# Choosing the tokens: one unit of the experts' first layer behind each block's gate products

## The reference

```python
gate_scores = softmax(x @ w_gate_w + w_gate_b)          # 8 experts
mask = one_hot(top_k(gate_scores, 2)).sum(-2)
masked = gate_scores * mask
route = masked / (masked.sum(axis=0) + EPS) * capacity  # over the 4 rows of the batch
_, seq_ids = top_k(route.transpose(2, 0, 1), S // 2)    # each expert takes 512 of 1024 tokens of a row
h = gelu(xg @ W1 + b1)                                  # 64 hidden numbers for each expert
o = h @ W2 + b2
outs = zeros.at[flat_ids].add(o)
```

## Time and profile before

| | |
|---|---|
| median of 3 runs | 3541.02 us (3540.13 to 3545.2) |
| profiled execution | 3554.61 us |
| its span, first to last instruction | 3552.9 us |
| mean granted clock of TensorE | 0.92 |
| TensorE (PE) busy | 3169.2 us, 89% |
| VectorE (DVE) busy | 2786.6 us, 78% |
| ScalarE (ACT) busy | 2104.8 us, 59% |
| `choose` in it | 3347.9 to 3463.2 us |
| `take` in it | 3463.2 to 3552.9 us |

### The profile page before, as it was taken

The page is one execution under the profiler, slowest core; times in us unless marked ns, Lnnn a source line. Parts: engine busy times, 40 slices in busy tenths (PEclk is TensorE's granted clock), DMA queues, the critical chain, the costliest instruction groups (busy, mean ns, idle before and its releaser), DMA issues. The chain is left out here.

```text
span 3552.9 us, 63589 instructions
## 1 busy us (share of the span) xinstructions
PE 3169.2 (89%) x23976; PEld 1628.0 (46%) x23976; DVE 2786.6 (78%) x4742; ACT 2104.8 (59%) x4195; POOL 870.6 (25%) x1299
## 2 busy tenths in 40 slices
PE   7599999678499879999999999999856699999699
PEld 4244444444288533333333333343345455454556
DVE  7688885447577898999999999999366677776456
ACT  3178887245333217999999999999815333334130
POOL 4234433134333430000000000000112334445100
PEclk9689999879699977999999999999978899999789
DMA  5422220000000330100100001000002410100001
GB/s 170 127 54 62 66 58 20 27 0 1 25 1 1 118 113 20 29 20 21 29 20 24 25 20 28 22 20 20 4 9 81 169 50 28 48 26 1 17 0 48
DMA packets 69587, 144.08 MB, mean 41 GB/s; under 512 B 20864, under 2 KB 33984, under 8 KB 69152
## 3 DMA queue, kind: packets, MB, share of 16 engines
q1 hardware_dynamic: 64928, 135.82, 12.9%
q10 hardware_dynamic: 4352, 4.20, 0.3%
HBM read 83.19 MB, written 54.53 MB: 39 GB/s over the span
## 5 line engine op out<-in xcount | busy, mean ns | idle before, releaser
L600 ACT ACTIVATE L_parts<-L_attn_psS 128x512 f32<-128x512 f32 (+3 forms) x2816 | 1410.3, 574 | 151.1 <-PE L_attn_psS L727 109.4
L683 DVE TENSOR_REDUCE L_attn_tops<-L_attn_psM 128x2 f32<-128x1024 f32 x1152 | 1326.4, 1218 | 62.4 <-PE L_attn_psM L777 59.1
L777 PE MATMUL L_attn_psM<-L_K,L_Q 30*128 30x512 f32 (+4 forms) x2816 | 869.0, 492 | 67.6 <-PEq L199 31.7
L727 PE MATMUL L_attn_psS<-L_Q,L_K 32*128 32x512 f32 (+4 forms) x2816 | 880.8, 477 | 1.6 <-ACT L_parts L600 0.9
L748 PE MATMUL L_attn_psS<-L_parts,L_attn_V 128*32 128x256 f32 (+1 forms) x10752 | 860.0, 392 | 5.5 <-ACT L_parts L600 0.6
L727 PEld LDWEIGHTS L_attn_psS<-L_Q,L_K 32*128 32x128 f32 (+1 forms) x2816 | 410.0, 186 | 558.8 <-ACT L_parts L600 274.4
L777 PEld LDWEIGHTS L_attn_psM<-L_K,L_Q 30*128 30x128 f32 (+1 forms) x2816 | 391.1, 190 | 114.3 <-DVE L_attn_tops L683 58.2
L748 PEld LDWEIGHTS L_attn_psS<-L_parts,L_attn_V 128*32 128x32 f32 x10752 | 215.0, 108 | 357.0 <-issue 189.0
L677 DVE CUSTOM_DVE_ANT_0 L_attn_psM<-L_attn_psM,L_attn_wide 128x384 f32<-128x384 f32 (+3 forms) x512 | 236.7, 523 | 20.2 <-PE L_attn_psM L777 19.7
L2357 ACT ACTIVATE x_E<-x_psS 128x512 f32<-128x512 f32 x256 | 139.0, 596 | 173.6 <-PE x_psS L2480 154.2
L2403 DVE TENSOR_REDUCE x_tops<-x_psM 128x2 f32<-128x1024 f32 x128 | 153.1, 1206 | 87.2 <-PE x_psM L2509 87.1
(11 more groups left out here) (370 smaller groups left out, 4083.6 us busy)
## 6 DMA issues: line engine op xcount, KB each, us to landing
parts_q<-L_parts SPq DMA_DIRECT2D x64, 256.0 KB
parts_k<-L_parts SPq DMA_DIRECT2D x64, 256.0 KB
L_Q<-parts_q SPq DMA_DIRECT2D x192, 64.0 KB
L_K<-parts_k SPq DMA_DIRECT2D x192, 64.0 KB
L_Q<-parts_q SPq DMA_DIRECT2D x64, 128.0 KB
L_K<-parts_k SPq DMA_DIRECT2D x64, 128.0 KB
queries<-x1p_qo SPq DMA_DIRECT2D x16, 512.0 KB, 3.8
keys<-x1p_ko SPq DMA_DIRECT2D x16, 512.0 KB, 4.2
```

The lines of the kernel that those rows point to most:

```text
L600: act.activation(E[(4 * n + s) % (4 * RING)][:, c0:], psS[bank][:, c0:], ACT.Exp, scale=scale).then_inc(e_done, 1)
L683: dve.tensor_reduce(dst, src, AX, ALU.max).then_inc(m_read, 1)
L727: pe.matmul(psS[bank][:, c0:], K[g.slot][r:r + RH, c, kt * P:(kt + 1) * P], Q[g.slot][r:r + RH, c, q * HALF + c0:(q + 1) * HALF], start=Tr ...
L777: last = pe.matmul(psM[bank][:, j * HALF:j * HALF + n], Q[t.slot][r:r + TOP, c, qt * P:(qt + 1) * P], K[t.slot][r:r + TOP, c, h * HALF:h * ...
```

## The change

One unit is issued behind each block's gate products, eight in all (`EARLY` = `NB`). These eight are written to the two banks of `psR` in turn instead of `psH`, as `psT` is in use by the turned blocks. From the third on each waits until ScalarE has put away the one of two units before it. `turned_routes` now waits until all eight are put away. The other 24 units follow as before: five between the two halves of the routes, 16 in the search, three behind it. ScalarE's queue puts each early Gelu behind the copy of the next block; the exponents of the first half stand between the copy of block 5 and the Gelu of unit 4, those of the second half behind the Gelu of unit 7.

```diff
+        EARLY = NB
+        hidden_bank = lambda n: psR[:, n % 2 * HALF:(n % 2 + 1) * HALF] if n < EARLY else psH[n % 4]
...
                 def hidden(n):
                     i, h = n // HC, n % HC
-                    if n >= 4:
+                    if n >= EARLY + 4:
 
                         pe.wait_ge(h_act, n - 3)
+                    elif 2 <= n < EARLY:
+                        pe.wait_ge(h_act, n - 1)
                     for c in range(DC):
-                        last = pe.matmul(psH[n % 4], w1[:, c, h * P:(h + 1) * P], XT[:, c, i * HALF:(i + 1) * HALF],
+                        last = pe.matmul(hidden_bank(n), w1[:, c, h * P:(h + 1) * P], XT[:, c, i * HALF:(i + 1) * HALF],
                                          start=(c == 0), stop=(c == DC - 1))
                     last.then_inc(h_pe, 1)
 
                 def turned_routes(h):
                     pe.wait_ge(done, (h + 1) * ROUTE)
+                    pe.wait_ge(h_act, EARLY)
...
                     if n + 1 < NB:
                         turned(n + 1)
                     gates(n)
+                    hidden(n)
                 turned_routes(0)
-                todo = iter(range(UNITS))
+                todo = iter(range(EARLY, UNITS))
...
+                def rectified(n):
+                    act.wait_ge(h_pe, n + 1)
+                    if n == 0:
+                        act.wait_ge(loaded, 112)
+                    act.activation(HT[:, n % HC, n // HC * HALF:(n // HC + 1) * HALF], hidden_bank(n), ACT.Gelu,
+                                   bias=b1[:, n % HC:n % HC + 1]).then_inc(h_act, 1)
...
-                for n in range(6):
-                    copied(n)
-                exponents(0)
-                for n in range(6, NB):
-                    copied(n)
+                copied(0)
+                for n in range(EARLY):
+                    if n + 1 < NB:
+                        copied(n + 1)
+                    if n == 4:
+                        exponents(0)
+                    rectified(n)
                 exponents(1)
...
-                for n in range(UNITS):
-                    act.wait_ge(h_pe, n + 1)
-                    act.activation(HT[:, n % HC, n // HC * HALF:(n // HC + 1) * HALF], psH[n % 4], ACT.Gelu,
-                                   bias=b1[:, n % HC:n % HC + 1]).then_inc(h_act, 1)
+                for n in range(EARLY, UNITS):
+                    rectified(n)
```

## The result

The changed kernel takes 3529.91 us (median of 8 runs, 3520.76 to 3534.08), the kernel before 3545.54 us beside it (8 runs, 3540.13 to 3553.11): 15.6 us less, ratio 0.9949 with a 95% interval of 0.9933 to 0.9965. The ratio goes by the means, which lie 18.1 us apart; in microseconds its interval is about 12 to 24. The forecast was 3525.8 us, in a range of 3520.5 to 3537, and 15.2 us less than before.

What follows compares the result with a forecast made beforehand. It took `choose` to be bound by TensorE at the low clock in the front and by leftover units in the tail. Terms -13.7 - 1.8 + 0.3 = -15.2 us from 3541.02 gave 3525.8 us, range 3520.5 to 3537.

Steps and rivals of the forecast that it cites:

- Term 1: Tail after the last count: eight units leave it at 1.72 us each, nearly all gained, -13.7 us.
- Term 2: Front of `choose`: seven added units, but the clock rises early and stays up; 36.5 us, -1.8 us.
- Both bounds: Front at full clock throughout, 31.7 us (-6.6), or at low clock throughout, 62.4 us (+24.1).
- Term 3: Between front and search: later exponents and routes, possible clock fall at the search's start; +0.3 us (bounds -1.5 and +3).
- Rival A: Clock rises and falls in the front, +8.7 us there; total 3536 us, chance 0.11.
- B: Clock stays low in the front, +24.1 us there; total 3552 us, chance 0.09.
- C: ScalarE bounds the front, or term 3 reaches its upper bound: +3 to +4 us, 3529 us, chance 0.10.

Runs made afterwards that it cites:

- e1: Kernel before, plus eight units behind the front's gate products with results thrown away and all 32 units kept: 3542.10 us, ratio 0.9998.
- e10: Changed kernel with eleven early units, two each behind blocks 5, 6 and 7: 3542.50 us, ratio 0.9983.
- e6: Changed kernel with 28 thrown-away transposes while TensorE waits for the weights: 3532.87 us, ratio 0.9961.
- e2: Changed kernel with gate products and transposes in turn and each unit split in two within a front block: 3560.41 us, ratio 1.0028.
- e4: Changed kernel with only the first four blocks followed by a unit (EARLY = 4): 3537.98 us, ratio 0.9969.
- e3: Kernel before with each block's eight transposes issued three times and no unit moved: 3545.74 us (one run).
- e7: Changed kernel with separate semaphores for the gate weights and the first layer's weights: 3524.55 us, ratio 0.9932.
- e8: e7 with the second half's exponents ahead of the eighth Gelu and both route halves turned behind the five units: 3529.57 us, ratio 0.9952.
- e9: e8 with four units before the turned routes and the fifth behind them, before the search's first sum: 3528.15 us, ratio 0.9939.
- e12: e9 with the two ScalarE bias copies for B2 moved from behind the eighth Gelu to behind the second: 3521.61 us, ratio 0.9934.

## Why the prediction was right

**The reading of the bound** (TensorE at the low clock in the front, twelve units in the tail, VectorE's steps in the search) was right by e1 and by the tail's 13.7 us.

**Term 1, -13.7 us:** 21.92 to 8.18 us, -13.74. That VectorE is next (7.5 us) was shown by e10, where three units less in the tail gained 0.36 us.

**Term 2, -1.8 us (bounds -6.6 and +24.1):** -1.2. The clock rose 10.1 us into the front ("some 10 us") and stayed up, and the price of the rise was 4.9 us (e6) for the 5 assumed. A block took 4.38 us for the 4.29 of the sum; 7 of these make the 0.6 us that the term was off. Both bounds were then produced: 59.8 us at the low clock (e2, with half a unit more in it; 62.4 in the sum) and 32.6 at the full (e6; 31.7). The choice between them was the forecast's risk, and its reason, the unbroken piece of unit and transposes, is borne out by e1, e2 and e4. e3 adds that no unit is needed for it.

**Term 3, +0.3 us:** the search began 13.77 us behind the last gate product in place of 13.26, +0.5; the exponents came 3.9 us behind it as forecast (3387.68 against 3383.82), the table load is 1.28 us and the exponent starts 20 ns behind it. So the drain that the Trainium skill adds ("ScalarE: Activation LUTs", section "What ACT_TABLE_LOAD costs") is not seen here either:

```profile
3386.38 1.28 ACT L2719 ACT_TABLE_LOAD   x1
...
3387.68 0.31 ACT L2719 ACTIVATE f_ex<-f_less 128x128 f32<-128x128 f32 x1
```

The search itself took 1.5 us less, as the clock did not fall in it in any of the three profiles of the changed kernel. The forecast had kept that loss as "a little more likely". So term 3 came out at -1.0 us in place of +0.3, the largest miss in the sum. The same idle time of 2.4 us before the first sum stands in twelve of the 14 profiles; nine show the fall behind it (before, e1 to e4, e6, e7, e8, e10), and the three of the changed kernel don't. Its line there:

```profile
3399.23 0.16 PE L2697 MATMUL f_psG<-f_flag,f_same_row 128*128 128x1 bf16 x1 [2.40 <-DVE f_flag L2812]
```

Why the changed kernel is spared stays open. The order of the instructions alone doesn't fix such changes of the clock: e7, e8, e9 and e12 begin the stage with the same 16 transposes, and in e12 the clock rose at their end, in the others only some 10 us into the front.

**The sum:** -13.7 - 1.2 + 0.5 - 1.5 = -15.9 us in the stage, against -15.2. Two misses of +0.6 and -1.3 us partly cancel. That the medians give 15.6 is closer than they can tell, with an interval of 12 to 24 us; so much of it is luck. The forecast's absolute time was 4.1 us too low, as the kernel before has a median of 3545.54 us in 8 runs and had 3541.02 in the three known then.

**Rival A** (up and down) did not occur in the changed kernel (e4 shows the fall when units are missing), **B** was the right picture of another order (e2), **C** was wrong: ScalarE is busy 16.03 of 37.43 us in the front, and PE never waits for it there.

**What the forecast got wrong in passing:** it looked for an effect of the later bias copies and GpSimd's subtraction only in `take`. In the changed kernel there was none, but the subtraction ended just 0.06 us before a cast of VectorE; in e8 and e9 the same subtraction cost 1.8 us.

## What to carry to other kernels

Where a stage has TensorE busy throughout and its granted clock at 0.50, try whether other products of the program can stand in one unbroken piece there: here seven units cost the front nothing, and in finer grain (e2) the front took 22 us more. When work is taken out of a tail, look which other engine ends next to it, and what TensorE does before the next stage: emptied entirely, the tail gave 0.4 us and `take` lost 6. Judge such changes by the stage in the profile, since the total of this kernel moves by 10 us and more from run to run.

## What the runs showed of the hardware

- Transposes alone can raise the granted clock: 24 in e3, from 0.50 to 1.00 at 3351.20. With 16 narrow products between each 24 they held it: 1.00 for 29.8 us. They don't always: eight to a block left it at 0.50 for the 38.7 us of the old front.
- A busy TensorE does not suffice: 59.8 us without idle time at 0.50 in e2, and a fall to 0.50 in e4 with no idle time at all.
- VectorE's cast of 128x32 waited for a running GpSimd subtraction: 1.97 us against 0.18 (e9, 1.96 in e8), and 0.18 again when the subtraction was moved (e12). The Trainium skill has this in "SBUF — State Buffer", section "Who interferes with whom": casts may use a pair of ports that VectorE shares with GpSimd, and who comes second waits for the whole instruction. The trace agrees.
